# New places for the stages of a chunk in each engine's order, and two weights centered earlier, in a one-core decoder layer

## What is computed

```python
# 1 selective state space ("mamba"); 256 channels, 16 states per channel
xb, z = split(x @ W_in);  xc = silu(causal_conv4(xb) + conv_b)
delta_raw, B, C = split(xc @ W_xproj);  delta = softplus(delta_raw @ W_dt + b_dt)
h[t] = exp(delta[t] * A) * h[t-1] + delta[t] * B[t] * xc[t]       # scan over t
y = (sum_s h[t, :, s] * C[t, s] + D * xc) * silu(z);  x1 = LN(x + y @ W_out)
# 2 retention over the context, rotary q and k, decay mask, no softmax
x2 = LN(x1 + ((rot(x1 @ Wq) @ rot(ctx @ Wk).T) * decay_mask) @ (ctx @ Wv))
# 3 mixture of 16 experts (top 2) plus a shared expert
hid_e = silu(x2 @ gate_e) * (x2 @ up_e)
out = LN(x2 + sum_e comb_e * (hid_e @ down_e) + shared(x2))
```

## Time and profile before

| | |
|---|---|
| time of the profiled execution | 1300.71 us |
| its span in the trace | 1298.7 us |
| DVE busy | 1174.9 us (90%) |
| PE busy | 1065.3 us (82%) |
| ACT busy | 939.8 us (72%) |
| POOL busy | 897.3 us (69%) |
| TensorE clock granted, mean | 0.962 |

### The profile page before, as it was taken

How to read it: one execution, slowest core, us unless ns; L and a number is a source line. 1 busy time by engine, 2 the same in 40 slices (tenths; PEclk the granted TensorE clock), 3 DMA queues, 4 the chain that set the end, 5 groups by cost and what they waited for, 6 DMA issues and landing times. The chain is left out here.

```text
span 1298.7 us, 18075 instructions
## 1 busy us (share of the span) xinstructions
PE 1065.3 (82%) x5959; PEld 733.0 (56%) x5959; DVE 1174.9 (90%) x1185; ACT 939.8 (72%) x2183; POOL 897.3 (69%) x556
## 2 busy tenths in 40 slices
PE   4476788888898878888887988888798888978877
PEld 2344455656565565656655665655666565556654
DVE  1999999999999999999999999999999999999621
ACT  4567768877777878777777787777778777777432
POOL 0567667778687777778767787877777787778533
PEclk7669799999999999999999999999999999999989
DMA  7334243343544444445444444454444444444112
GB/s 177 141 104 168 100 163 133 127 174 132 180 144 167 136 148 150 144 168 172 142 159 145 145 149 152 165 170 149 131 150 145 160 153 169 143 143 166 40 45 73
DMA packets 77149, 185.83 MB, mean 143 GB/s; under 512 B 15848, under 2 KB 43904, under 8 KB 60672
## 3 DMA queue, kind: packets, MB, share of 16 engines
q1 hardware_dynamic: 77056, 184.68, 42.4%
HBM read 178.88 MB, written 5.77 MB: 142 GB/s over the span
## 5 line engine op out<-in xcount | busy, mean ns | idle before, releaser
L811 POOL TENSOR_TENSOR read<-state,bc_all 128x1024 f32<-128x1024 f32 x256 | 603.5, 2360 | 258.7 <-DVE state L761 257.3
L761 DVE TENSOR_TENSOR_SCAN state<-decay,drive_bank 128x1024 f32<-128x1024 f32 x256 | 584.5, 2283 | 12.4 <-POOL read L811 0.3
L606 ACT ACTIVATE decay<-delta,a_neg 128x252 f32<-128x252 f32 x1024 | 422.8, 496 | 0.6
L244 PE MATMUL y_bank<-ident,read 128*128 128x128 f32 x2048 | 282.6, 283 | 85.2 <-POOL read L811 84.9
L644 DVE TENSOR_TENSOR drive_bank<-dx_bank,bc_all 128x1024 f32<-128x1024 f32 x256 | 314.8, 1230 | 24.6 <-DMA bc_all<-bc_dram 14.7
L244 PEld LDWEIGHTS y_bank<-ident,read 128*128 128x128 f32 x2048 | 237.3, 145 | 163.0 <-POOL read L811 139.1
L840 POOL TENSOR_TENSOR hid<-gu,comb_all 128x512 f32<-128x512 f32 x128 | 162.3, 1274 | 34.7 <-DVE gu L776 17.4
L583 ACT ACTIVATE silu<-bank 128x512 f32<-128x512 f32 x144 | 85.7, 595 | 135.7 <-PE bank L240 134.4
L240 PE MATMUL bank<-x2T,up_w 128*128 128x512 f32 x256 | 133.8, 604 | 16.7 <-DVE conv L616 12.7
L240 PEld LDWEIGHTS down_bank<-down_w,hid 128*128 128x128 f32 x1024 | 127.7, 193 | 34.8 <-issue 26.8
L240 PE MATMUL down_bank<-down_w,hid 128*128 128x128 f32 x1024 | 138.6, 279 | 3.7 <-POOL hid L840 1.7
(11 more groups left out here) (123 smaller groups left out, 1418.4 us busy)
## 6 DMA issues: line engine op xcount, KB each, us to landing
bc_all<-bc_dram SPq DMA_DIRECT2D x128, 1024.0 KB, 5.0
comb_all<-comb_dram SPq DMA_DIRECT2D x256, 128.0 KB, 5.0
x_in<-in_x_dram SPq DMA_DIRECT2D x16, 256.0 KB, 5.4
ctx_in<-in_ctx_dram SPq DMA_DIRECT2D x16, 256.0 KB, 5.3
out_dram<-y_out SPq DMA_DIRECT2D x16, 256.0 KB, 2.6
bc_dram<-proj SPq DMA_DIRECT2D x16, 64.0 KB, 4.3
gate_w<-in_L_ffn_gate_proj_dram SPq DMA_DIRECT2D x1, 512.0 KB, 4.7
up_w<-in_L_ffn_up_proj_dram SPq DMA_DIRECT2D x1, 512.0 KB, 6.6
```

What stands on the lines that cost most here:

```text
L244: return e.matmul(out, in_, identity[0:n, 0:n], is_transpose=True, start=start, stop=stop, skip_group_check=True)
L606: done = e.activation(seqs(decay_t[j % DECAYS][:, i, h, :])[:, :, 1:T], seqs(delta[c % 2][:, h, sub * SUB:(sub + 1) * SUB])[:, :, 1:T], AC ...
L761: e.tensor_tensor_scan(flat(state_t[j % STATE_BUFS][:, :, :, :]), flat(decay_t[j % DECAYS][:, :, :, :]), flat(drive_bank[:, :, :, :]), 0.0 ...
L811: e.tensor_tensor(read_t[j % READS][:, :, :, :], state_t[j % STATE_BUFS][:, :, :, :], bc_all[group % BC_BUFS][:, 1, PAIR * i:PAIR * (i + 1 ...
```

## The change

Nearly all `where` numbers move by one to twelve slots, on every engine. The numbers that the prediction speaks of, and the weights:

```diff
-        EXP_AT = [11, 28]
+        EXP_AT = [10, 26]
-        FFN_AT = [70, 72, 73, 74, 78, 84, 86, 87, 90]
+        FFN_AT = [70, 72, 74, 76, 78, 84, 86, 86, 90]
...
-                if (c := chunk_at(slot, -18)) is not None:
+                if (c := chunk_at(slot, -17)) is not None:
                     w.wait_ge(S["conv_tap"], at(c, 5, 6))
...
                     e.activation(xc[c % 2][:, :, :], conv[:, :, :], ACT.Silu, scale=1.0).then_inc(S["xc"], 1)
...
+                for part, at_slot, centered in (
+                        (0, -1, ((w_out[:, :, :], 0, HALVES), (down_w[:, :, :], HALVES, PAIRS))),
+                        (1, 3, ((w_qkv[:, 2:3, :], HALVES + PAIRS, 1), (shared_w[:, 2:3, :], HALVES + PAIRS + 1, 1)))):
+                    if slot != at_slot:
+                        continue
+                    if part == 0:
+                        w.wait_ge(S["out_consts"], 16 * 2)
+                    else:
+                        w.wait_ge(S["flip_copy"], 2)
...
+            e.dma_start(x_t[1][:, :, :], x_view[1]).then_inc(S["x_load1"], 16)
+            e.dma_start(w_out[:, :, :], io["L0_attn_W_out"].rearrange("(h p) n -> p h n", p=P)).then_inc(S["out_consts"], 16)
+            e.dma_start(down_w[:, :, :], io["L0_ffn_down_proj"].rearrange("k e d -> (k e) d").rearrange(
+                "(j p) d -> p j d", p=P)).then_inc(S["out_consts"], 16)
             e.dma_start(xpos[:, :, :], io["c_xpos"]).then_inc(late, 16)
```

More of the change, by code:

```diff
@@ L248, in _ @@
                 k = slot
-                if (c := chunk_at(slot, -24)) is not None:
+                if (c := chunk_at(slot, -23)) is not None:
                     if c == 0:
@@ L258, in _ @@
                     bank.free = (S["xT"], at(c))
-                for h, where in enumerate((-22, -19)):
+                for h, where in enumerate((-22, -21)):
                     if (c := chunk_at(slot, where)) is not None:
@@ L280, in _ @@
                         bank.free = (S["delta"], at(c, h, 2))
-                for sub, where in enumerate((5, 26)):
+                for sub, where in enumerate((7, 25)):
                     if (c := chunk_at(slot, where)) is not None:
@@ L304, in _ @@
                     bank.free = (S["flip_copy"], 3)
-                if (c := chunk_at(slot, 30)) is not None:
+                if (c := chunk_at(slot, 28)) is not None:
                     bank = take(("ctxT", c), slot, 1)
@@ L350, in _ @@
                     bank.free = (NORMED[LN1], at(c))
-                if (c := chunk_at(slot, 43)) is not None:
+                if (c := chunk_at(slot, 41)) is not None:
                     bank = take(("x1T", c), slot, 1)
@@ L374, in _ @@
                     bank.free = (S["ret"], at(c))
-                if (c := chunk_at(slot, 53)) is not None:
+                if (c := chunk_at(slot, 55)) is not None:
                     bank = take(("retout", c), slot, 4.5)
@@ L385, in _ @@
                     bank.free = (NORMED[LN2], at(c))
-                if (c := chunk_at(slot, 59)) is not None:
+                if (c := chunk_at(slot, 60)) is not None:
                     bank = take(("x2T", c), slot, 1)
@@ L401, in _ @@
                     bank.free = (S["router"], at(c, 0, ROUTER))
-                if (c := chunk_at(slot, 69)) is not None:
+                if (c := chunk_at(slot, 68)) is not None:
                     bank = take(("combT", c), slot, 1)
@@ L445, in _ @@
                         continue
+                    w.wait_ge(S["centered"], 2)
                     if index == 0:
@@ L494, in _ @@
                                          S["conv_bias"], 1)
-                if (c := chunk_at(slot, -15)) is not None:
+                if (c := chunk_at(slot, -16)) is not None:
                     w.wait_ge(S["proj_mm"], at(c))
@@ L661, in _ @@
                         tap(c, h, 3)
[L663 to L673, removed]
+                for part, at_slot, centered in (
[6 more added lines that the diff above has]
+                    else:
+                        w.wait_ge(S["flip_copy"], 2)
+                        for i in range(2):
+                            from_pairs, to_pairs = (a[:, i, :].rearrange("p (n two) -> p n two", two=2)
+                                                    for a in (w_qkv, w_swap))
+                            for side in (0, 1):
+                                done = e.tensor_copy(to_pairs[:, :, side], from_pairs[:, :, 1 - side])
+                        done.then_inc(S["swap"], 1)
+                    first, last = centered[0][1], centered[1][1] + centered[1][2]
                     for weights, i, n in centered:
@@ L694, in _ @@
                 for i in range(2):
-                    if (c := chunk_at(slot, 50 + i)) is not None:
+                    if (c := chunk_at(slot, 49 + i)) is not None:
                         w.wait_ge(S["q_mm"], at(c, i, 2))
@@ L822, in _ @@
                                         ALU.mult).then_inc(S["dx"], 1)
-                if (c := chunk_at(slot, 36)) is not None:
+                if (c := chunk_at(slot, 48)) is not None:
                     w.wait_ge(S["k_rot"], at(c, 1, 2))
@@ L888, in _ @@
             for slot in range(FIRST, LAST + 1):
-                if (c := chunk_at(slot, -10)) is not None:
+                if (c := chunk_at(slot, -15)) is not None:
                     w.wait_ge(S["proj"], at(c))
@@ L903, in _ @@
                                     BC_LOAD[group % BC_BUFS], 16)
-                if (c := chunk_at(slot, 67)) is not None:
+                if (c := chunk_at(slot, 68)) is not None:
                     w.wait_ge(S["combT"], at(c))
```

77 lines of the change are left out of this document (37 added, 40 removed).

## The result

The changed kernel took 1357.8 us (median of four runs, 1355.64 to 1359.8), the kernel before 1300.11 us (four runs): a ratio of 1.0443, with a 95% interval of 1.0423 to 1.0463. The forecast was 1325 us and slower; the direction held, the size was 25 us against 57.7, and the time lies outside the range of 1297 to 1343.

A forecast was written before the change was run, and what follows sets the result against it. DVE was taken as the bound, almost never waiting between first and last scans. 1300.71 + 0.5 + 33.8 − 6.4 − 3.4 = 1325.2 us profiled; 0.7 lower for the median gives forecast 1325, range 1297 to 1343.

The forecast's parts named there:

- Head: Before scan 1: centering partly moved earlier, but ACT's weight copies come later, so scan 1 starts at 42.2 against 41.70: +0.5 us.
- Middle: Between first and last scans: 54 added ACT table loads make DVE wait 2.35 us per window in 13 windows: +33.8 us.
- The waits for silus: In each middle window, DVE waits 1.3 us ahead of tile 4's `gu` and 0.3 us ahead of tile 5's.
- The wait ahead of `ret`: In each middle window, late `xc` delays PE's products and the scores, so DVE waits 0.75 us.
- The small DVE instruction: Router's `TENSOR_SCALAR` L744 on DVE moves past the end of POOL's `read` and becomes short: −6.4 us over 14 windows.
- Tail: Kernel end: two down products and ACT's router Exp reordered, shorter wait for POOL's `hid`: −3.4 us, bounds −5 and 0.
- the fully exposed loads: Rival for the middle: table loads reach DVE nearly in full, up to 5.1 us per window, 1360 us; chance 0.06.
- the drain behind a switch: ACT table switches: the skill's added DRAIN of about 1380 ns was not seen in the trace and was left out.

## Why the prediction was wrong

- **Head, +0.5**: the chain was right. The copies came late as counted, DVE waited 3.80 us, its swap began at 40.58 (40.7) and scan 1 at 42.12 (42.2). The size is no test, though: in the nine profiles with this head, the changed kernel and its variants, scan 1 started at 41.95 to 42.12 in six and at 39.85 to 40.34 in three, with the first drive as much earlier.
- **Middle, +33.8**: right in mechanism, as the run with Copy in place of Silu shows, and too small by 5.9 against the 39.7 measured. Two parts missed in opposite directions. The waits for silus came out smaller: per window 1.3 us were forecast ahead of tile 4, the wait of tile 3 inside them, and 0.3 ahead of tile 5; measured were 0.27 + 0.82 at 683 and 690 us, and nothing ahead of tile 5. With the last window that is 16.7 in place of 24.0. The wait ahead of `ret` came out larger: 0.75 forecast, 0.99 measured where TensorE's clock held, 2.4 to 2.6 in the windows where it did not, 22.5 in all in place of 9.8. The step left out was the clock: the prediction put 1.84 us for the product behind `xc` though it had itself worked out that PE would wait there. In the six long windows that is some 9.4 us; with the pause filled, this wait fell by 8.0 (22.5 to 14.5).
- **The small DVE instruction, −6.4**: the step that failed. Its own instruction moved as forecast, −6.6 us. But the mechanism, read rightly from the earlier trace rows, was applied to the one instruction that was long before, and not to all that the change moves: `masked` and `soft<-top` now stand beside a `read`, +28.1 us. For `soft<-top` the order shown ahead of the prediction had it: it stands between the two `k_rot`, where the long TENSOR_SCALAR had stood. The term should have been +21.5. Its bounds, 0 and −7, held no such case; neither did any rival.
- **Tail, −3.4**: right, −3.7 (83.1 against 86.8 from the last scan on), and in its parts: the last `combT` copy on ACT comes 49.7 us behind the last scan where it came 51.9 behind, 2.2 earlier as forecast, and the remaining 1.5 us lie behind it (1.2 forecast).
- **Rivals**: the fully exposed loads gave 1360, near the time and for another reason: their waits never came near 69 us, and the rest is the router's; that it lies near is luck. On the drain behind a switch: none is seen in the changed kernel either. A silu ends at 683.42, its load runs from 683.43 to 684.71, the next Exp starts at 684.73. ACT's 1014.7 us are 939.8 plus 54 loads of 1.28 and 5.8 us more, which no run explains.

Sum by the measured terms: 0.4 + 39.7 + 23.3 − 3.7 = 59.7, against 58.4 for the spans; the terms make 1.3 us too much, which stay unassigned.

## What to carry to other kernels

When an engine is full, look at the mean duration of every small instruction on it, not only at its waits: an instruction that is held counts as busy. A new order must be checked for each small instruction with its inputs in SBUF against what POOL runs there, the newcomers above all; the fix for one can push the next into the same hole. And a table of slots is one thing: one row of it put back can make a wait of its own. Where effects don't add up, compare the granted clock window by window: here the same pause cost a wait of 1.0 or of 2.6 us, in six, eight or nine windows by the variant.

## What the runs showed of the hardware

- DVE and POOL exclude each other for some forms. Held to the end of POOL's operation: TENSOR_TENSOR and SCALAR_TENSOR_TENSOR with two SBUF inputs, also when they write PSUM, and TENSOR_SCALAR and COPY from SBUF to SBUF of 128x64 (1.8 us each in place of about 0.2). Not held: TENSOR_REDUCE, a product with one input in PSUM, RECIPROCAL of 128x4 (0.15 to 0.21). Beside a TENSOR_SCALAR of POOL (1.05 us) a product of two SBUF tiles was held too (0.57). The Trainium skill says as much in "GPSIMD Engine Reference", section "Specifications": the SBUF interfaces are shared, with contention for DVE instructions "in a 2-port perf mode or with two SBUF inputs". For two SBUF inputs the runs agree; whether TENSOR_SCALAR and COPY ran in such a mode no view shows. The price here is the rest of POOL's operation, up to 2 us for 64 columns.
- It goes both ways: where a DVE operation with two SBUF inputs was next in line when POOL started, POOL's 2.34 us became 2.65 and 3.05, longer by the 0.3 and 0.7 us for which DVE was still busy with the instruction ahead. TENSOR_SCALAR and COPY in the same position waited themselves (2.08 and 1.68 us).
- POOL's power operation of 128x4 (1.01 us, from 622.56 in the kernel before) did not hold the router's `comb` and `masked` (0.22 and 0.23 us, from 622.95 and 623.21).
- Behind one and the same pause of 2.58 us TensorE's granted clock was 1.00 in seven windows from 200 us on and a mix with half of it in six, and the same four matmuls took 1.88, 2.63 and 3.33 us. The length of the pause alone doesn't decide: behind 1.78 us they were slow in ten windows of 13, behind 0.21 to 0.65 us in none. What does decide between the windows no run shows.
- The granted clock also fell with at most 0.2 us of pause just ahead, behind the product that reads 8 rows of `proj` (0.50 to 0.70 over 3 us): in one window of 13 in the kernel before, in four and in seven in two of the variants. In each of them DVE waited 1.2 to 1.6 us for a bank.
